# Layer 0's gate, up and router products from split operands, with a smaller set of buffers

## The reference, cut to what matters

```python
logits = x @ gate_w.T                      # router, 8 experts
scores = jax.nn.sigmoid(logits)            # groups, top 4, weights cw
g = jnp.einsum('nh,ehi->eni', x, Wg)       # gate, 256 -> 128 for each of 8 experts
u = jnp.einsum('nh,ehi->eni', x, Wu)       # up
y = jnp.einsum('eni,eih->enh', jax.nn.silu(g) * u, Wd)
routed = jnp.einsum('enh,ne->nh', y, cw)
out = routed + _mlp(x, Wg_s, Wu_s, Wd_s)   # a ninth, shared expert
```

## Time and profile before

| | us |
|---|---|
| median of 3 runs | 1029.98 |
| lowest and highest of them | 1029.2 and 1030.4 |
| the profiled execution | 1034.0 |
| its span, first to last instruction | 1032.1 |
| PE busy | 923.3 (89%) |
| DVE busy | 749.5 (73%) |
| ACT busy | 486.5 (47%) |

### The profile page before, as it was taken

How to read it: one execution, slowest core, us unless ns; L and a number is a source line. 1 busy time by engine, 2 the same in 40 slices (tenths; PEclk the granted TensorE clock), 3 DMA queues, 4 the chain that set the end, 5 groups by cost and what they waited for, 6 DMA issues and landing times.

```text
span 1032.1 us, 18031 instructions
## 1 busy us (share of the span) xinstructions
PE 923.3 (89%) x6385; PEld 737.4 (71%) x6385; DVE 749.5 (73%) x1494; ACT 486.5 (47%) x842; POOL 242.0 (23%) x390
## 2 busy tenths in 40 slices
PE   5578899999999999999989788786599999999995
PEld 3355677777767666776766555554599999999995
DVE  2345676777676768988888889757688888888882
ACT  2125544443444443443433444431276666677662
POOL 5011210120201000111010133320434444444433
PEclk9557999999999999999999866765599999999998
DMA  5766896254161444547363873430577667777642
GB/s 153 151 123 123 170 209 106 65 90 80 41 104 43 69 102 86 105 116 136 100 133 94 222 167 90 117 87 22 190 241 235 206 208 225 228 232 233 208 144 30
DMA packets 129866, 141.52 MB, mean 137 GB/s; under 512 B 12561, under 2 KB 122281, under 8 KB 129649
## 3 DMA queue, kind: packets, MB, share of 16 engines
q1 hardware_dynamic: 119296, 127.59, 49.4%
q0 software_dynamic: 8832, 12.25, 5.5%
q10 hardware_dynamic: 1648, 0.53, 0.3%
HBM read 109.45 MB, written 30.36 MB: 135 GB/s over the span
## 4 chain that ended last, share of the span: by engine, by line
PE 66%; DVE 19%; issue 4%; ACT 3%; POOL 2%; DMA 2%; SPq 1%; POOLq 0%; DVEq 0%; ACTq 0%
PE bank L966 12%; PE bank L802 9%; PE by_query L950 7%; PE by_key L950 6%; DVE rowmax L1295 5%; PE bank L812 5%; PE value_bank L744 4%; PE bank L650 4%; PE by_query L707 3%; PE bank L693 3%; DVE probs L1320 3%; PE by_key L726 2%; PE bank L659 2%; PE bank L771 2%; DMA lower<-lower 2%
## 5 line engine op out<-in xcount | busy, mean ns | idle before, releaser
L1295 DVE TENSOR_REDUCE rowmax<-by_query 128x4 f32<-128x1024 f32 x128 | 155.6, 1216 | 20.2 <-PE by_query L707 20.1
L1102 ACT ACTIVATE probs<-by_key 128x1024 f32<-128x1024 f32 x128 | 130.7, 1021 | 46.3 <-PE by_key L726 43.3
L1788 POOL TENSOR_SCALAR rstd<-moments 128x2 f32<-128x2 f32 x32 | 10.5, 328 | 526.5 <-DVE moments L1254 526.5
L1848 POOL DMA_INDIRECT out_x<-x,token_i x46 | 78.2, 1699 | 146.6 <-ACT x L1205 136.7
L966 PE MATMUL bank<-w_hi,h_hi 128*128 128x256 f32 x368 | 104.1, 283 | 0.0
L966 PE MATMUL bank<-w_lo,h_hi 128*128 128x256 f32 x368 | 104.1, 283 | 0.0
L966 PE MATMUL bank<-w_hi,h_lo 128*128 128x256 f32 x368 | 104.1, 283 | 0.0
L707 PE MATMUL by_query<-stack_k,stack_q 48*128 48x256 f32 x512 | 70.5, 357 | 30.6 <-DVE rowmax L1295 30.1
L1135 ACT ACTIVATE act_gate<-bank 128x256 f32<-128x256 f32 x72 | 27.6, 383 | 141.5 <-PE bank L802 139.0
L707 PEld LDWEIGHTS by_query<-stack_k,stack_q 48*128 48x128 f32 x512 | 42.9, 206 | 70.0 <-DVE rowmax L1295 39.2
L1320 DVE SCALAR_TENSOR_TENSOR probs<-probs,lower 128x1024 f32<-128x1024 f32 x64 | 78.1, 1220 | 11.5 <-DMA lower<-lower 6.7
(11 more groups left out here) (242 smaller groups left out, 2143.7 us busy)
## 6 DMA issues: line engine op xcount, KB each, us to landing
w<-in_L_ffn_W SPq DMA_DIRECT2D x46, 1024.0 KB, 8.9
lower<-lower SPq DMA_DIRECT2D x64, 256.0 KB, 5.4
stack_k<-qk SPq DMA_DIRECT2D x96, 128.0 KB, 5.2
stack_q<-qk SPq DMA_DIRECT2D x96, 128.0 KB, 6.8
qk<-hi SPq DMA_DIRECT2D x31, 256.0 KB, 2.6
qk<-lo SPq DMA_DIRECT2D x31, 256.0 KB, 2.7
rows<-w_gate SPq DMA_DIRECT2D x8, 264.0 KB, 4.8
x<-in_x SPq DMA_DIRECT2D x8, 256.0 KB, 6.4
```

What stands on the lines that cost most here:

```text
L1102: ac.activation(probs[i % 4][:, :, :, :].rearrange("p k h s -> p h k s"), by_key[:, :, :].rearrange("p h (k s) -> p h k s", k=2), ACT.Exp) ...
L1295: dv.tensor_reduce(rowmax[u % 2][:, :, p, :], by_query[:, :, :].rearrange("p h (t s) -> p h t s", t=TT), AX, ALU.max).then_inc(sem.max_don ...
L1848: po.indirect_dma_start(out[:, :], bass.IndirectOffsetOnAxis(ap=token_i[:, n:n + 1].bitcast(U32), axis=0), ysb[i % 3][:, t, :], None, comp ...
```

## The change

Layer 0's router, gate and up products are formed from split operands, as layer 1's mixture does it:

- ACT's copy of the transposed bank rounds it to `x_hi`; a new DVE stage, `x_low`, subtracts it from the bank to give `x_lo`, one half slot after `turn`. The bank is free only after that. There is one pair `x_hi`, `x_lo` for all batches, so ACT's copy waits for all nine `gate_up` of the batch before.
- `route0` has 12 products in place of 4, and `gate_up` has 12 in place of 4. `route0` and what follows it on DVE come one half slot later, and both wait for `x_lo`.
- The weights are split once, in batch 0: `split_expert`, for each of nine experts two roundings on ACT and two subtractions on DVE, two half slots before the expert's first `gate_up`. The low parts take the place of the loaded weights.
- The router's weights are split in the same way (`gate_turn`, once).
- Beside them: `hidden0` has four buffers in place of six; the value products (PE L744) write 17 rows in place of 32 for each head, with `value_bank` cleared once; two of the `lower` buffers share their place with `ctx_tok`, so SP's first two loads of `lower` wait for the store of `zalt`; several semaphores are merged and count by two.

```diff
@@ make_plan
+        at[e + 5 + EXPERTS0_STEP * n // N0].append(("split_expert", n))
-        at[e + 6].append(("route0", b))
-        at[e + 8].append(("groups0", b))
+        at[e + 6].append(("x_low", b))
+        at[e + 7].append(("route0", b))
+        at[e + 9].append(("groups0", b))
@@ bank_release
-        return "xnT_ready", NORM_NO[n] + 1
+        return ("x_lo", n[1] + 1) if n[0] == "ffn0" else ("xnT_ready", NORM_NO[n] + 1)
@@ PE
-                    mm = pe.matmul(value_bank[32 * c:32 * c + 32, o:o + S], values[u % 2][:, kt, 4 * j + c, :],
+                    mm = pe.matmul(value_bank[32 * c:32 * c + HD + 1, o:o + S], values[u % 2][:, kt, 4 * j + c, :],
 def route0(b):
-            pe.wait_ge(sem.xnT_ready, no + 1)
+            pe.wait_ge(sem.x_lo, b + 1)
+            products = [(xt, wt, k) for k in range(KC) for xt, wt in ((x_hi, gate_hi), (x_hi, gate_lo), (x_lo, gate_hi))]
 def gate_up(i):
+                pe.wait_ge(sem.w0_lo, n + 1)
+            pe.wait_ge(sem.x_lo, b + 1)
-            for half, w in enumerate((w_gate0, w_up0)):
-                for k in range(KC):
-                    mm = pe.matmul(bank[:, half * S:half * S + S], w[:, k, e, :], turned_of(("ffn0", b))[:, k, :],
+            for half, (hi, lo) in enumerate(((w_gate_hi, w_gate_lo), (w_up_hi, w_up_lo))):
+                products = [(wt, xt, k) for k in range(KC) for wt, xt in ((hi, x_hi), (hi, x_lo), (lo, x_hi))]
@@ ACT
-            elif kind == "ffn0" and n >= 2:
-                ac.wait_ge(sem.gu_done, N0 * (n - 1))
+            elif kind == "ffn0" and n:
+                ac.wait_ge(sem.gu_done, N0 * n)
+        def split_expert(n):
+            ac.wait_ge(expert_in[n % 3], 48 * (n // 3 + 1))
+            for hi, raw in ((w_gate_hi, w_gate0), (w_up_hi, w_up0)):
+                op = ac.activation(hi[:, :, e, :], raw[:, :, e, :], ACT.Copy)
@@ DVE
+        def split_expert(n):
+            dv.wait_ge(sem.w0_hi, n + 1)
+            for lo, hi, raw in ((w_gate_lo, w_gate_hi, w_gate0), (w_up_lo, w_up_hi, w_up0)):
+                op = dv.tensor_tensor(lo[:, :, e, :], raw[:, :, e, :], hi[:, :, e, :].bitcast(F32), ALU.subtract)
+        def x_low(b):
+            dv.wait_ge(sem.xnT_ready, NORM_NO[norm] + 1)
+            dv.tensor_tensor(x_lo[...], banks[BANK_OF["turn", norm][0]][:, :], x_hi[...].bitcast(F32), ALU.subtract)
-            if i >= 6:
-                dv.wait_ge(sem.y_done, i - 5)
+            if i >= HIDDEN:
+                dv.wait_ge(sem.y_done, i - HIDDEN + 1)
@@ SP
+            if j < 2:
+                sp.wait_ge(sem.zalt_out, 16)
```

More of the change, by code:

```diff
@@ L291, in build @@
     shiftT = sba("shiftT", [3 * H * TT, P])
-    lower = [sba(f"lower{i}", [P, 2, S]) for i in range(3)]
+    lower = ctx_or_lower + [sba("lower2", [P, 2, S])]
     probs = [sba(f"probs{i}", [P, 2, 2, S]) for i in range(4)]
@@ L301, in build @@
     wT = sba("wT", [E1, TT * P])
-    hidden0 = [sba(f"hidden0_{i}", [P, S]) for i in range(6)]
+    hidden = sba("hidden0", [P, HIDDEN, S])
+    hidden0 = [hidden[:, i, :] for i in range(HIDDEN)]
     act_gate = [sba(f"act_gate{i}", [P, S]) for i in range(2)]
@@ L309, in build @@
     gate_rows = hidden0[2][0:E0, :]
-    vm, zalt = (ctx_tok[i][0:NB, :, :].rearrange("p t c -> p (t c)")[:, 0:D] for i in range(2))
+    vm, zalt = (t[0:NB, 0, :] for t in ctx_or_lower)
     vmT = sba("vmT", [P, KC, NB])
@@ L376, in turned_of @@
         kind, n = norm
[L377 removed]
+        if kind == "ffn0":
+            return x_hi
+        if kind == "finish" and n % 3:
+            return hidden[:, 2 * (n % 3) - 2:2 * (n % 3), :]
+        return xnT0
     def x_ready(engine, kind, n):
```

104 lines of the change are left out of this document (60 added, 44 removed).

## The result

The changed kernel took 1035.28 us (median of 4 runs, 1034.7 to 1036.9) against 1029.74 us (4 runs, 1029.2 to 1030.4) before: a ratio of 1.0056, 95% interval 1.0039 to 1.0074. Ratios and intervals leave out the runs that fell into a second, slower state; medians of the experiments are over all runs. So it is 0.3 to 0.6% slower, where 1.5% faster was forecast, and the time lies outside the range of 1004 to 1028. The profiled execution took 1035.68 us with a span of 1033.9.

The account below looks back on a forecast made before the run. PE was taken to bound the kernel from 125 to 395 us, alternating with DVE afterwards. Savings of 2 (batch 0), 1.6 (batch 1), 9 (2 to 4) and 2.4 (5 to 7) gave 15.0 us: 1029.98 to 1015 us, range 1004 to 1028.

Parts of the forecast that it names:

- PE's saving of 24 us: Layer 0's mixture on PE: 3.45 us less gate_up, 0.44 more router a batch; net 3.0, over eight batches 24 us.
- the 1 us charged to batch 0: Batch 0 on DVE: weight splits queue ahead of maxima and hidden0; charged 1 us, leaving 2 us saved there.
- the new wait: PE's router waits for x_low behind the keys' low part: 1.4 us in batches 1 and 5, none in 2 to 4.
- PE is the bound, and what is taken from it shortens the span: From 125 to 395 us PE is busy 266.9 of 270 us, its largest sum of waits 1.0 us, for row maxima.
- The price of `gate_up`: On PE, twelve products at 0.12 us plus 0.1 for entry: 1.54 us against 1.93, saving 27.6 us in all 72.
- The router: On PE, twelve records take 1.33 us in place of 0.89: 0.44 us more a batch, 3.5 in all.
- The value products: On PE, 17 rows written in place of 32: taken as 0 saved, upper bound below 3 us over 64 calls.
- What DVE gets: x_low 0.69 us a batch, 5.5 in all; 18 weight low parts of 0.43 us, 7.7 in all, in batch 0.
- inside the 1 us: Batch 0: the fifth expert's load may just miss its earlier use; that loss was counted within batch 0's charge.
- the prediction's own signs of being wrong: PE waiting for xnT_lo in every batch, clock leaving 1.00 before 395 us, or over 5 us shortening after 395 us.
- DVE takes over: Rival: DVE's added work lands on its path in batch 0 and after 395 us; 6.6 us saved, 1023 us, chance 0.20.
- the clock falls: Rival: a 1.4 us wait and a clock fall in every batch, 3.0 us each, eat PE's saving; 1040 us, chance 0.10.

Follow-up runs that it names:

- one_product: Changed kernel with gate_up forming hi x hi alone, four products in place of twelve (output differs): 1023.1 us, ratio 0.9899.
- buffers_only: Changed kernel without the split: plain products, old plan places; smaller buffers, 17-row value products and merged semaphores stay: 1030.24 us, ratio 0.9996.
- early_split: Changed kernel with the experts' weights loaded and split 24 half slots earlier: 1040.87 us, ratio 1.0114.
- order_twice: Repeat of order_mended, the same kernel, beside the changed kernel: 1025.59 us, ratio 0.9940.
- loads_earlier: order_twice with the experts' loads from the fourth on planned two half slots earlier, SP waiting for ACT's rounding: 1022.26 us, ratio 0.9921.
- order_mended: Changed kernel with x_low first in its half slot and the router's groups, ranks and weights back in their old half slots: 1029.31 us, ratio 0.9971.

## Why the prediction was wrong

**Which steps failed.** The sum was PE's saving of 24 us less 9.0 us for DVE (1 in batch 0, 1.4 in batch 1, 6.6 in batches 5 to 7), with nothing for the clock: 15 us. In the same terms the runs gave 18.9 us of saving, 10.5 us more idle, and 11.2 us of PE's busy time to the clock. So the largest miss is a term that stood at nothing, the clock (11.2 us); then the saving, 5.1 too high; then the idle time, 1.5 too low in all but at other places than named. Two steps on DVE's side were wrong as well, the 1 us charged to batch 0 and the moved chain, which had no term; they and the new wait made the long pauses. Mending these, the place of `x_low` and the loads made the kernel 13 us faster without touching the products.

**What bounds the kernel.** "PE is the bound, and what is taken from it shortens the span" held for a part of what was taken. PE's waits of 1.0 us in the first stretch say how little it waits now, not how far behind DVE is. The `hidden0` that ended at 138.0 was already late by 0.28 us. one_product shows the margin: 68 us less for PE, 13.4 us less in the stretch. (The page's row was also read a little high: PE is at 9 tenths in slices 6 to 20 and in 22, not from 5 to 22.)

**The price of `gate_up`: mis-sized.** 1.61 us, not 1.54. The pitch of 0.12 us was right, the cost of entering and leaving was taken once at 0.1 and is nearer 0.2. The saving is 0.31 us in place of 0.38 to 0.39, 22 us in place of 27.6. The formula in the Trainium skill, TensorE: Matmul & The Clock Gate, section Back-to-back issue gap, which holds there for an isolated gap and not for a stream with weight loads, gave the prediction an estimate of 1.31 us; the trace has 1.61.

**The router: right.** 0.45 us more by medians, 0.44 in batch 1, as forecast. Net on PE some 19 us in place of 24, all of the difference from `gate_up`.

**The value products, the buffers:** nothing, as forecast (0.99 us for sixteen records; buffers_only).

**What DVE gets.** The durations were right (0.68 and 0.42 us; forecast 0.69 and 0.43). "I charge 1 us" to batch 0 was the largest miss in a single batch: it lost 4.3 us where 2 were to be won. The splits and loads in the middle of it are 1.3 of the 6.3 (early_split); the chain queued behind the wait for ACT and the fall behind the pause are in the rest. The late load, "inside the 1 us", held ACT for 5.8 us. It cost batch 0 2.1 us once the order was mended (order_twice to loads_earlier, 53.3 to 51.2 us); what it cost in the changed kernel itself is not shown.

**The moved chain: priced at nothing, without being named.** That the router's chain comes one half slot later was listed with the change, and the prediction gave it no term. It counted the new DVE operations and not the old ones that changed their place against a wait. It cost 2.4 to 2.7 us in each of batches 4 to 6, two thirds of it by way of the clock.

**The new wait.** Right in place and size (1.2 and 1.3 us, forecast 1.4, none in 2 to 4). Not counted was the fall of the clock behind it, 1.0 us in batch 1.

**The clock** was a rival at 0.10 with a price of 3 us a batch, and stood at nothing in the sum. It asked for a pause in every batch. In the changed kernel four pauses of 1.2 to 2.1 us, two of them at places that the prediction didn't name, each had a fall behind them before 395 us, which is one of the prediction's own signs of being wrong. The Trainium skill, same page, section A second HAM failure mode: psum-queue depth-cycling, says that frequent short idles between groups of matmuls make the clock drop and return; the trace of order_twice agrees, with a fall behind three waits of 0.5, 0.35 and 0.34 us. That "three waits for maxima of up to 0.4 us left the clock at 1.00" was no evidence on pauses three times as long. The price of a short fall was 1.0 to 1.1 us in batch 1, 1.4 and 1.5 where PE's idle time stayed the same (two in batch 0 of order_mended, one in batch 4 of order_twice), against the 1.6 forecast (1.7 by the prediction's own 0.86 us for that half of a `gate_up` behind `down0`).

**The sum.** In us, against the kernel before:

| batches | forecast | changed | loads_earlier |
|---|---|---|---|
| 0 | -2 | +4.3 | -0.1 |
| 1 | -1.6 | -0.8 | -1.8 |
| 2 to 4 | -9 | -0.8 | -4.7 |
| 5 to 7 | -2.4 | +0.3 | -3.3 |
| stretch | -15 | +2.8 | -10.2 |

| | forecast | changed | loads_earlier |
|---|---|---|---|
| PE's work | -24 | -18.9 | -18.9 |
| PE's busy time by the clock | 0 | +11.2 | 0 |
| PE idle | +9.0 | +10.5 | +8.6 |

The work is taken from loads_earlier, which has as much half clock as the kernel before, and the clock's term is the rest of the busy time. The three terms are what PE did, not three separate causes: without a fall PE is sooner at the next buffer, and where DVE is late part of what the clock gives back becomes waiting (0.3 of 1.4 us in batch 1, all of it in batch 5).

"DVE takes over" (1023 us, 0.20) and "the clock falls" (1040 us, 0.10) each had a part of it; the first loss was not after 395 us but in batch 0, and falls came although not every batch had a pause. That the order on DVE and the late loads cost most of the 13 us is shown by edits: 8.6 with order_mended's 428.5, 11.5 with order_twice's 425.6, each with the 2.1 us of batch 0's load. The rest are falls that one profile has and the other has not. That the fall behind a pause goes when the pause is filled is shown for the two ahead of the routers. What decides a fall elsewhere stays open: waits of 2.1, 1.5, 1.2 and 0.5 us had one behind them in one run and, within 0.1 us of that length, none in another. That each of DVE's late `hidden0` is decided by its place in the queue is shown for batch 0 and for batch 4, and argued for 5 and 6.

## What to carry to other kernels

When work is taken from the busiest engine, price what its partner does in the same slots: follow the chain that frees the buffer the faster engine will ask for, and see how late it is already. A stage that is moved by one slot "to make room" is an edit of its own: short operations that ran in the idle time ahead of a wait stand behind it afterwards, with all that is queued there. Give the clock a term of its own as soon as the change makes the busiest engine pause, and compare its busy time at equal work: here that was the larger part of what a mended order gave back. And if a new step uses loaded data earlier, plan the load earlier by as much; here the three together turned 0.3 to 0.6% slower into 0.8% faster without touching the products.
